# A graph network kernel: the edge softmax runs along partitions, and a short stage joins runs across them

## The reference, cut to what matters

```python
q = (x @ Wq + bq); k = (x @ Wk + bk); v = (x @ Wv + bv)     # [N, 8, 16] each
e = (edge_attr @ We)
k_j = k[src] + e
v_j = v[src] + e
logits = jnp.sum(q[dst] * k_j, axis=-1) / np.sqrt(C)
m = segment_max(logits, dst); ex = jnp.exp(logits - m[dst])
denom = segment_sum(ex, dst); alpha = ex / denom[dst]
agg = segment_sum(alpha[..., None] * v_j, dst)
h = _ln(agg + x @ Wskip + bskip + x, g1, b1)                # then a feed-forward block
```

## Time and profile before

| | |
|---|---|
| median of 3 runs | 4584.0 us (4579.99 to 4588.58) |
| the profiled execution's own time (its span) | 5458.0 us |
| stages in the profile: sort, message passing, last layer, attention, feed-forward | 745, 1438, 890, 1395, 862 us |
| mean granted TensorE clock | 0.88 |

### The profile page before, as it was taken

The page is one execution under the profiler, slowest core; times in us unless marked ns, Lnnn a source line. Parts: engine busy times, 40 slices in busy tenths (PEclk is TensorE's granted clock), DMA queues, the critical chain, the costliest instruction groups (busy, mean ns, idle before and its releaser), DMA issues. The chain is left out here.

```text
span 5458.0 us, 111849 instructions
## 1 busy us (share of the span) xinstructions
PE 4332.6 (79%) x23759; PEld 2886.3 (53%) x23858; DVE 3587.2 (66%) x12001; ACT 2141.5 (39%) x4806; POOL 2901.1 (53%) x2863
## 2 busy tenths in 40 slices
PE   5666664888867888689999967777777775999998
PEld 2444443666645666556666635555555553444444
DVE  7566653444434444478888847667766765899998
ACT  0222221444433444323333323232323332777777
POOL 0555555555535555354444335555555553777775
PEclk9888887999979999989999977777877777999999
DMA  0333334666646666568888744444544443444443
GB/s 18 125 123 131 127 126 119 189 192 186 188 139 184 188 190 189 172 195 266 266 262 264 241 154 134 131 134 130 143 132 129 135 132 92 117 125 128 126 128 99
DMA packets 693097, 852.73 MB, mean 156 GB/s; under 512 B 149445, under 2 KB 511032, under 8 KB 692916
## 3 DMA queue, kind: packets, MB, share of 16 engines
q1 hardware_dynamic: 580020, 631.94, 35.7%
q0 software_dynamic: 112896, 218.94, 16.7%
HBM read 451.91 MB, written 398.61 MB: 156 GB/s over the span
## 5 line engine op out<-in xcount | busy, mean ns | idle before, releaser
L760 POOL DMA_INDIRECT mp_gathered<-msg_rows,other_idx x784 | 752.4, 960 | 659.0 <-PE bank L776 211.1
L776 PE MATMUL bank<-mp_edge_hot,mp_gathered 128*128 128x256 bf16 x3528 | 539.7, 282 | 203.1 <-issue 166.0
L1066 POOL DMA_INDIRECT ll_gathered<-msg_rows,other_idx x392 | 376.1, 959 | 479.1 <-PE bank L1085 228.8
L526 POOL DMA_INDIRECT by_window<-so_pay,so_pos_i x392 | 397.7, 1015 | 435.5 <-issue 299.0
L1372 POOL DMA_INDIRECT at_kv<-kv_rows,kv_idx x392 | 375.6, 958 | 456.3 <-PE bank L1403 176.4
L776 PEld LDWEIGHTS bank<-mp_edge_hot,mp_gathered 128*128 x3528 | 349.8, 99 | 349.2 <-issue 294.3
L879 DVE TENSOR_TENSOR mp_msg_out<-mp_rest,mp_msg_out 128x256 bf16<-128x256 f32 x392 | 166.8, 425 | 490.5 <-ACT mp_msg_out L837 290.7
L824 ACT ACTIVATE mp_h_out<-bank,mp_b_agg 128x256 f32<-128x256 f32 x392 | 185.8, 474 | 714.5 <-PE bank L794 321.6
L1670 POOL DMA_INDIRECT ff_agg<-at_rows,last_idx x392 | 385.8, 984 | 115.9 <-issue 103.0
L1374 POOL DMA_INDIRECT at_q<-q_rows,node_idx x392 | 371.8, 948 | 130.2 <-issue 130.2
L856 DVE TENSOR_SCALAR mp_edge_hot<-digits,mp_first_col,column 128x256 bf16<-128x256 bf16 x1176 | 346.7, 357 | 80.3 <-issue 62.0
(11 more groups left out here) (258 smaller groups left out, 10199.2 us busy)
## 6 DMA issues: line engine op xcount, KB each, us to landing
msg_rows<-mp_msg_out SPq DMA_DIRECT2D x392, 192.0 KB
mp_h_in<-h_cols SPq DMA_DIRECT2D x392, 128.0 KB
h_cols<-mp_h_out SPq DMA_DIRECT2D x392, 128.0 KB
kv_rows<-ll_proj SPq DMA_DIRECT2D x98, 512.0 KB
msg_rows<-so_msg_out SPq DMA_DIRECT2D x98, 384.0 KB
h_cols<-so_h_out SPq DMA_DIRECT2D x98, 256.0 KB
ll_h_in<-h_cols SPq DMA_DIRECT2D x196, 128.0 KB
x_rows<-ll_x_b SPq DMA_DIRECT2D x98, 256.0 KB
```

The lines of the kernel that those rows point to most:

```text
L526: pool.indirect_dma_start(core.by_window, bass.IndirectOffsetOnAxis(ap=pos_i[k][:, t:t + 1], axis=0), pay[k][:, t, :], None, bounds_check= ...
L760: pool.indirect_dma_start(gathered[:, r * PARTS * D:(r + 1) * PARTS * D], None, core.msg_rows[layer % 2], bass.IndirectOffsetOnAxis(ap=cor ...
L776: product = nc.tensor.matmul(agg_bank[k], gathered[:, bass.ds(at + d * D, D)], hot, start=(first and d == 0), stop=True, skip_group_check= ...
L1066: pool.indirect_dma_start(gathered[:, r * PARTS * D:(r + 1) * PARTS * D], None, core.msg_rows[(LAYERS - 1) % 2], bass.IndirectOffsetOnAxis ...
```

## The change

Edge n now sits on partition n // 392 at place n % 392 (NT = 392). A partition holds 392 sorted edges, and a run of one target lies along the free axis of the layout in which gathered rows arrive. The index tables are loaded in this order. In `attention`:

- The transposes of logits, values and sums go, with the pick product, the filler matmuls, the spreading and the flags' loads. A break table for all groups is made once, from `joins`.
- The softmax state is one number per head. The maximum and the denominator are scans of 128x40: 8 heads of SLOT = 5 places, where place 0 carries the last group's state and the scan restarts. Only the numerator is wide (128x640: 128 features of 5 places). Operands that are read or written per edge in it have a step of 5 floats.
- One Exp makes both factors (64 numbers a partition), one ACT copy spreads the decay to 128x640.
- A stored row has ROW = 144 floats: the average, the 8 maxima and the 8 denominators.
- POOL's gathers keep their count and size; they wait for products and values of g-4 only. SP's loop is written out; attributes come in pieces of 1 KB a partition by two DMAs.

A new stage `join_runs` corrects the first run of each partition where it goes on from the one before: it loads the last row of each partition, gathers the last row of each partition's first run, transposes both (features to partitions), scans 128 partitions' states, and scatters 128 corrected rows back into `at_rows`. `feed_forward` gathers rows of 144 floats and uses 128 of them.

```diff
@@ sort_by_window
-        src_i, dst_i, part_i = sb("so_src_i", [P, T, P], I32), ...
-                for f, i in zip(parts_f, (win_i, col_i, dst_i, src_i)):
-                    nc.vector.tensor_copy(f[:, :, :], i[:, :, :]).then_inc(flt, 1)
...
+                load_runs(sp, core.kv_idx, src, loaded)
+                load_runs(sp, core.node_idx, dst, loaded)
+                    sp.dma_start(before_i[1:P, :], dst[0:(P - 1) * NT].rearrange("(p j) -> p j", j=NT)[:, NT - 1:NT]).then_inc(loaded, 16)
...
+                nc.vector.tensor_tensor(core.joins[:, 1:NT], core.node_idx[:, 1:NT], core.node_idx[:, 0:NT - 1], ALU.is_equal).then_inc(tab, 1)
-            def _(pe):
-                        last = nc.tensor.transpose(bank[c][:, b * P:(b + 1) * P], tile[:, b, :], core.ident[:, :])
@@ attention, POOL and PE
                 reached(pool, prod_ok, g - DEEP + 1)
                 reached(pool, ve_ok, g - DEEP + 1)
-                reached(pool, e_mm, g - DEEP + 2)
...
             def turn(do):
-                do(2, turn_attr)
-                do(1, edge_features)
-                do(-1, turn_values)
-                do(-2, turn_back)
+                do(3, turn_attr)
                 do(0, skip_product)
-                do(0, turn_logits)
+                do(3, edge_features)
@@ attention, ACT
+            def factors(g, k, i):
+                nc.scalar.activation(factor[k][:, :, :, 1:SLOT].rearrange("p a h j -> p (a h) j"),
+                                     gap[k][:, :, :, :].rearrange("p a h j -> p (a h) j"), ACT.Exp, scale=-SCALE).then_inc(f_ok, 1)
+            def decays(g, k, i):
+                nc.scalar.activation(decay[k][:, :, :].rearrange("p (h c) j -> p h c j", h=H),
+                                     factor[k][:, 1, :, :].unsqueeze(2).broadcast_to([P, H, C, SLOT]), ACT.Copy).then_inc(dec_ok, 1)
@@ attention, DVE
+            def weigh(g, k, i):
+                nc.vector.tensor_tensor(wv[k][:, :, 1:SLOT].rearrange("p (h c) j -> p j h c", h=H),
+                                        v_e[k][:, :, :].rearrange("p j (h c) -> p j h c", h=H),
+                                        factor[k][:, 0, :, 1:SLOT].rearrange("p h j -> p j h").unsqueeze(3).broadcast_to([P, J, H, C]), ALU.mult)
+            def num_scan(g, k, i):
+                nc.vector.tensor_tensor_scan(num[k][:, :, :].rearrange("p f s -> p (f s)"), decay[k]..., wv[k]..., 0.0, ALU.mult, ALU.add)
+            def carry_num(g, k, i):
+                nc.vector.tensor_copy(wv[(k + 1) % DEEP][:, :, 0], num[k][:, :, J]).then_inc(nc_ok, 1)
...
             def turn(do):
+                do(0, values)
+                do(-1, weigh)
+                do(0, keys)
+                do(-1, num_scan)
+                do(0, products)
+                do(-1, den_scan)
                 do(0, edge_logits)
+                do(-1, carry_num)
+                do(-1, inverses)
+                do(0, maxima)
+                do(0, gaps)
+                do(0, carry_top)
+                do(-1, averages)
@@ build
         attention(core, a["edge_attr_64"], l1, l1)
         core.end_stage()
+        join_runs(core)
+        core.end_stage()
         feed_forward(core, l1, out)
```

More of the change, by code:

```diff
@@ L41 @@
 FAR = 65536
+ROW = D + 2 * H
 BIG = 3.0e38
@@ L238, in _ @@
                 sp.wait_ge(filled, 3)
[L239 to L247, removed]
+                load_runs(sp, core.kv_idx, src, loaded)
+                load_runs(sp, core.node_idx, dst, loaded)
+                with nc.allow_non_contiguous_dma(reason="the target before each partition's first edge"):
+                    sp.dma_start(before_i[1:P, :], dst[0:(P - 1) * NT].rearrange("(p j) -> p j", j=NT)[:, NT - 1:NT]).then_inc(loaded, 16)
             @block.vector
             def _(dve):
[L251 to L254, removed]
+                nc.vector.memset(core.kv_idx[:, :], NP - 1).then_inc(filled, 1)
+                nc.vector.memset(core.node_idx[:, :], NP - 1).then_inc(filled, 1)
+                nc.vector.memset(before_i[:, :], NP).then_inc(filled, 1)
                 nc.vector.memset(ones_col[:, :], 1.0)
@@ L1274, in deep @@
             return [sb(f"{name}{k}", shape, dt) for k in range(DEEP)]
[L1275 to L1278, removed]
+        w_e = sb("we", [ED, D])
@@ new lines, in attention @@
+        brk = sb("break", [P, NG * FLAT])
+        logits, top_den = two("logits", [P, H, SLOT]), two("top_den", [P, 2, H, SLOT])
+        drop, gap = sb("drop", [P, H, J]), two("gap", [P, 2, H, J])
+        factor, decay = two("factor", [P, 2, H, SLOT]), two("decay", [P, D, SLOT])
+        wv, num, inv = two("weighted", [P, D, SLOT]), two("num", [P, D, SLOT]), two("inv", [P, H, J])
+        rows, zero_rows = deep("rows", [P, J, ROW]), sb("zero_rows", [P, ROW])
+        in_run, runs = sb("in_run", [P, NT - 1]), sb("runs", [P, 8])
@@ L1282, in attention @@
[L1282 to L1296, removed]
@@ L1341, in store @@
[L1341 to L1353 removed]
+                for lo, hi in ((0, SPLIT), (SPLIT, last)):
+                    sp.dma_start(attr[k][lo:hi, :, :], bass.AP(edge_attr.tensor, edge_attr.offset + (lo * NT + g * J) * ED,
+                                                              [[NT * ED, hi - lo], [ED, J], [1, ED]])).then_inc(a_in[k], 16)
@@ L1354, in _ @@
+            for n in range(-5, NG + 4):
+                for lag, step in ((5, load), (3, load_cols), (-1, store_skip), (-3, store)):
+                    if 0 <= n + lag < NG:
+                        step(n + lag)
+            sp.wait_ge(zero_st, 32)
             for k in range(DEEP):
@@ L1494, in _ @@
+            def turn(do):
+                do(3, attr_copy)
+                do(0, factors)
+                do(0, decays)
+                do(0, skip_copy)
+                do(-1, states)
             turns(act, turn, DEEP, 8)
@@ new lines, in _ @@
+            dve.wait_ge(based, 2)
+            nc.vector.tensor_scalar(whole, length, float(NT - 1), None, ALU.is_equal).then_inc(run_c, 1)
+            nc.vector.tensor_tensor(runs[:, 2:3], length, base_f[:, 0:1], ALU.add).then_inc(run_c, 1)
+            dve.wait_ge(run_c, 4)
+            nc.vector.tensor_tensor(core.through[:, :], whole, joined, ALU.mult).then_inc(run_c, 1)
+            nc.vector.tensor_tensor(runs[:, 3:4], runs[:, 2:3], base_f[:, 1:2], ALU.subtract).then_inc(run_c, 1)
+            dve.wait_ge(run_c, 6)
```

491 lines of the change are left out of this document (281 added, 210 removed).

## The result

The changed kernel takes 4640.4 us (median of 4 runs, 4638.0 to 4646.7), beside 4582.9 us (4580.0 to 4588.6) for the kernel before: ratio 1.0131 [1.0116, 1.0145], slower by 57 us. I had forecast 4500. A pair in square brackets behind a ratio is its 95% interval.

What follows compares the result with a forecast made beforehand. Attention was taken as bound by a round trip through DVE, ACT, PE and POOL, afterwards by POOL's gathers. Attention -101, join_runs +18 and sort -4 took 4584 to 4497, forecast 4500 us, range 4300 to 4575.

Steps and rivals of the forecast that it cites:

- attention after: Attention in the changed kernel: 2.7 + 982 + 2 + 8.5 + 3.7 = 999 us.
- POOL is then never held: Attention: POOL's gathers never wait for products while DVE's turn is under 10 us; 784 gathers take 982 us.
- the middle of two bounds: Timed attention before: between POOL's floor with its ends, 1029, and its share of the median, 1172; taken as 1100 us.
- rival (c): Attention already at POOL's floor in a timed run; the change gives nothing, 1029 to 999 and +14: 4568 us; chance 0.07.
- The step of 5 floats: DVE's weigh, averages and carry_num: no cost, 0.69 us; upper bound a scan's pace, 1.23 us, +1.1 us a group.
- Rival (d): Attention: the 20 byte step makes DVE the bound, deciding from a turn of 10.9 us; slower, 4661 us; chance 0.11.
- The numerator scan: DVE in attention: grown to 640 places at 2.14 ns a place and 0.13 fixed, 1.50 us.
- PE's cold clock: PE in attention: working three groups ahead, so neither its length nor a cold clock is on the path.
- the sort: Sort stage: transposes, casts and one store's operations go; 4 us off, bounds +2 and -7.
- feed-forward's wider rows: Feed-forward: gathers rows of 576 and not 512 B; nothing, bound +10.
- the ends of attention: Around POOL's gathers: 2.7 us ahead; 2 landing, 8.5 for one turn and a half, and 3.7 behind.
- Rival (a): POOL's 0.30 us between gathers is wholly or partly the tracing's; DVE's 8.0 decides, attention 830, time 4333 us; chance 0.14.

Runs made afterwards that it cites:

- e_all_psum: Changed kernel with decay, values and inverses in PSUM, edge features in one bank and one group ahead, skip product in one bank: 4553.9 us.
- second profile: The kernel before, unchanged, profiled once more: execution 4591.3 us, span 4589.2 us.
- e_contig: Changed kernel with neighbours of weigh's output and averages' input 4 bytes apart, not 20, so the scan sums misplaced numbers: 4607.8 us.
- e_values_psum: Changed kernel with values and inverses in PSUM, the decay still in SBUF: 4649.6 us.

## Why the prediction was wrong

The miss is 140 us. By the profiles it is made of these terms: attention after, 1088.5 and not 999 (+89.5); attention before, 1045 and not 1100 (+55); join_runs 15.4 and not 18 (-2.6); ahead of attention -6.0 and not -4 (-2); feed-forward -1.4 and not 0. Together 138.5.

**The step that failed: "POOL is then never held, and it is what is late next: 784 x (0.953 mean + 0.30) = 982 us".** POOL is the bound, as said, and never waits for products, as said; but the gather's 0.953 us is no constant of the instruction. It is 1.061 in the changed kernel, because DVE holds the gathers up. I took a duration from one neighbourhood (operations with a PSUM operand) into another (operations with two SBUF operands) and asked only whether POOL would wait for a semaphore. This one error, 79 us more on POOL than in the kernel before, turned the forecast gain into a loss. The rest of the stage's sum holds: with the collisions gone, e_all_psum's attention takes 1001.7 us against the 999 that I had worked out.

The Trainium skill has a rule that fits, and I missed it: "SBUF — State Buffer", section "SBUF: two separate sides", says that DVE and GpSimd share one pair of SBUF ports as an exclusive lock, that a DVE operation with two SBUF inputs takes it against a GpSimd operation that reads SBUF, and that the later of the two is blocked until the first has ended. The runs agree that the gather waits until the DVE operation has ended. The section doesn't say that an indirect gather is such a GpSimd operation; the runs show that it behaves like one. Of the other way round they show little: weigh takes 1.07 us in the mean where it starts inside a gather, as elsewhere, and 1.12 to 1.13 where the gather starts within 0.03 us behind its start; that gather isn't held. In the prediction I weighed another section of that page. A count of wide DVE operations with two SBUF operands in the diff (from `at_drop` and its kind to weigh, numerator scan and averages) would have put a chance on this outcome.

**The length of attention before.** I took the middle of two bounds, 1029 and 1172, for no reason but that it is the middle, and 1045 lies close to the lower. The premise of rival (c) (before, attention was already at POOL's pace) was right and I gave it 0.07. The case for it stood in the earlier trace rows: a DVE turn of 9.7 us below POOL's 10.0. The 456 us of POOL's idle time and the 321 us ahead of the maximum scan were counted as causes, though the same execution was 874 us too long. POOL's idle time between gathers makes nearly all of what attention was too long by: 586 us there and 239 in the second profile, in stages of 1395 and 1045. I also misread its row: 176 of the 456 us are charged to L1403, not most of them, and 113 to values. With 1045 in place of 1100 my own sum gives 4584 - 46 + 18 - 4 = 4552, and e_all_psum measured 4553.9.

**The step of 5 floats "at no cost".** It costs 0.38 us in each wide operation, inside my bounds (0.69 to 1.23); I took the wrong end. I argued that this is harmless as long as DVE stays under POOL's pace. DVE's turn is 706.7 / 98 = 7.2 us busy, under the 8.0 that I took, with 3.7 us idle, and yet the step costs some 33 us of the time. The rule of the Trainium skill that the prediction cites, "SBUF — State Buffer", section "Door 1: The DMA port swizzle", was right in sign: e_contig puts a size to it.

**Rival (d).** Slower, at 4661, is near the result and for the wrong reason: it wanted a DVE turn of 10.9 us.

**What was right.** The numerator scan at 1.475 us (1.50); PE's cold clock: granted 0.50, the 1.2 GHz level, in attention where it was 0.86, the feature matmuls at 437 ns instead of 307, and off the path (3.4 us of DVE's 362 are charged to PE); the sort, whose count starts 7.7 us earlier (14.4 us, before 22.1 in the second profile); join_runs (the reciprocal's price a place is 6.25 ns by the two rows cited, not 6.4, which changes nothing); feed-forward's wider rows at nothing; and the ends of attention, 17.5 us around POOL's gathers for my 17, with some luck: 0.7 us ahead of them where I had 2.7, and 17 behind where I had 14. Rival (a) is excluded: the timed executions are as long as the profiled ones, in which 784 gaps of 0.305 us are part of the stage.

## What to carry to other kernels

A duration read from a trace belongs to its neighbours as well as to its instruction: when a change moves DVE operands from PSUM to SBUF while POOL gathers, count the operations with two SBUF inputs and price each collision on POOL. Removing transposes through PSUM removes such cover too; putting all of the wide operations' second operands back in PSUM gave 86.5 us, putting back some gave nothing, so test such a fix whole. Two SBUF inputs are not the only case: a copy between SBUF tiles held gathers up too. And profile once more when a profiled execution is much longer than the timed ones, before any of its waits is taken for a cause.

## What the hardware showed that I had not expected

- An indirect DMA on POOL that starts while a DVE operation with two SBUF operands runs ends 0.69 to 0.83 us after that operation's end (0.69 to 0.71 behind weigh, 0.75 to 0.77 behind the scans, 0.82 to 0.83 behind the added addition), and so takes up to 1.75 us in the changed kernel's turns (2.21 in e_values_psum) where it takes 0.945. With one operand in PSUM, a DVE operation of the same kind and length does nothing to it. All are f32.
- Operations with one SBUF input or none can do it too. The copy of 128x128 between SBUF tiles holds up 7 gathers of e_all_psum, by up to 0.11 us. Ahead of DVE's first turn, the gather that starts at 2680.32 in the changed kernel takes 3.80 us and ends 0.82 us behind the end of the break table's L1446, an operation with one tensor input that starts 1.2 us after it, behind a memset; every kernel with the new layout has one such gather there, of 3.65 to 3.81 us. Which of the two operations holds it was not tested. A reduction of 128x512 with one SBUF input holds up none.
- The cost is not additive. The collisions of two operations out of three, or one out of three, cost as much as all three (4641, 4650, 4640 us); none cost 86.5 less. That DVE's phase follows the arriving rows is the likely reason; it was not tested by moving the phase alone.
- Once DVE's turns run, who starts first decides, and the border is sharp: in the changed kernel gathers that start ahead of weigh, or up to 0.03 us behind its start, take 0.94 to 0.95 us; those that start 0.04 us behind it take 1.72. In the other kernels the border lies between 0.01 and 0.1 us behind the operation's start.
- 128x512 f32 with a step of 20 bytes on one side takes 1.06 to 1.07 us, with 4 bytes 0.68 to 0.69.
- Two executions of one kernel under the profiler had spans of 5458.0 and 4589.2 us, and only the second looks like the timed ones. What stretched the first is open.
